# A four-layer GNN stack on one core: a new order of items on four engines, new PSUM banks and other bank waits

## What is computed

```
x = LN(x + L0(x))   # 8-head attention (head size 64); adj and exp(-adj) are added to the softmax, each times 0.33
x = LN(x + L1(x))   # hypergraph convolution 256 -> 512, ReLU, layer norm, convolution 512 -> 256, residual
x = LN(x + L2(x))   # gated diffusion: transition = adj*exp(leaky_relu(sj+si)), normalised;
                    # H = x@Wk0 + T x@Wk1 + T T x@Wk2 + biases, ReLU
x = LN(x + L3(x))   # mean over neighbours, concatenated with x, times W, ReLU
```

## Time and profile before

| | |
|---|---|
| median of three runs | 1284.12 us |
| the profiled execution | 1283.25 us |
| its span | 1281.4 us |
| PE matmul busy | 1231.0 us (96%), 9397 instructions |
| PE weight load busy | 1092.4 us (85%) |
| DVE busy | 1109.5 us (87%) |
| ACT busy | 959.2 us (75%) |
| POOL busy | 488.3 us (38%) |
| DMA | 45.14 MB, 35 GB/s over the span |
| PE's share of the chain that ended last | 80% |

### The profile page before, as it was taken

The page is one execution under the profiler, slowest core; times in us unless marked ns, Lnnn a source line. Parts: engine busy times, 40 slices in busy tenths (PEclk is TensorE's granted clock), DMA queues, the critical chain, the costliest instruction groups (busy, mean ns, idle before and its releaser), DMA issues.

```text
span 1281.4 us, 32306 instructions
## 1 busy us (share of the span) xinstructions
PE 1231.0 (96%) x9397; PEld 1092.4 (85%) x9397; DVE 1109.5 (87%) x3463; ACT 959.2 (75%) x2774; POOL 488.3 (38%) x1126
## 2 busy tenths in 40 slices
PE   4799999999999999999999999999999999999985
PEld 4588889888888888888988888898888898888874
DVE  3779889899889998988999998899898899999885
ACT  3567777778777777777777877778787777787773
POOL 2234333334343334433333444333443333344432
PEclk9889999999999999999999999999999999999998
DMA  8111101111110111111111111011111101111000
GB/s 227 30 23 40 39 21 26 30 38 38 38 28 25 28 32 38 38 38 21 25 30 38 38 38 29 25 28 32 38 38 38 23 23 30 38 38 30 16 10 9
DMA packets 146696, 45.14 MB, mean 35 GB/s; under 512 B 110577, under 2 KB 145521, under 8 KB 146673
## 3 DMA queue, kind: packets, MB, share of 16 engines
q1 hardware_dynamic: 142976, 43.81, 14.9%
q10 hardware_dynamic: 3520, 0.54, 0.3%
q0 software_dynamic: 176, 0.52, 0.2%
...
## 4 chain that ended last, share of the span: by engine, by line
PE 80%; DVE 6%; ACT 5%; issue 4%; POOL 3%; ACTq 2%; POOLq 0%; DVEq 0%
PE PS L434 13%; PE PS L435 13%; PE PS L438 13%; PE PS L563 5%; PE PS L553 5%; PE PS L509 4%; PE PS L543 4%; PE PS L510 4%; PE PS L513 4%; PE PS L598 3%; PE PS L612 2%; ACT mbc L864 2%; POOL rs L1720 1%; DVE ysb L1445 1%; ACT qk L875 1%
## 5 line engine op out<-in xcount | busy, mean ns | idle before, releaser
L1714 POOL TENSOR_TENSOR rs<-mv,eps_c 128x1 f32<-128x1 f32 x256 | 51.9, 203 | 640.3 <-DVE mv L1205 640.3
L1720 POOL TENSOR_TENSOR rs<-rs,mhalf 128x1 f32<-128x1 f32 x320 | 175.9, 550 | 25.4
L892 ACT ACTIVATE prob<-PS,neg_max 128x128 f32<-128x128 f32 x512 | 179.7, 383 | 2.0 <-DVE neg_max L1277 2.0
L509 PE MATMUL PS<-xT_hi,wqk_hi 128*128 128x256 f32 x512 | 144.5, 304 | 4.6 <-ACT wv_hi L837 4.6
L1290 DVE SCALAR_TENSOR_TENSOR prob<-prob,rl,gate 128x128 f32<-128x128 f32 x512 | 143.7, 342 | 0.1
L510 PE MATMUL PS<-xT_hi,wqk_lo 128*128 128x256 f32 x512 | 135.6, 286 | 0.0
L892 ACT ACTIVATION_READ_ACCUMULATOR prob<-PS,neg_max 128x1 f32 x512 | 114.3, 223 | 0.0
L509 PEld LDWEIGHTS PS<-xT_hi,wqk_hi 128*128 128x128 f32 x512 | 98.7, 193 | 9.9 <-issue 5.1
L1727 POOL TENSOR_SCALAR rs<-mv,rs 128x1 f32<-128x1 f32 x256 | 84.1, 329 | 53.1 <-POOL rs L1720 53.1
L513 PE MATMUL PS<-xT_lo,wqk_hi 128*128 128x256 f32 x512 | 103.9, 285 | 0.0
L510 PEld LDWEIGHTS PS<-xT_hi,wqk_lo 128*128 128x128 f32 x512 | 99.4, 194 | 0.0
...
## 6 DMA issues: line engine op xcount, KB each, us to landing
...
ablk<-in_adj_dram SPq DMA_DIRECT2D x128, 32.0 KB, 1.9
...
```

The source lines that it names most:

```text
L509: pe.matmul(dst, w[0], xT0[0][:, c], start=(c == 0), stop=False)
L892: last = act.activation(prob[:, t, h, :], PS[:, bank, k * P:(k + 1) * P], ACT.Exp, bias=neg_max[:, t, h:h + 1], accum_out=row_sum[:, t, h: ...
L1720: return pool.tensor_tensor(rs[:, n, g, 1:2], rs[:, n, g, 0:1], mhalf[:], ALU.pow)
```

## The change

It rewrites the order of items in `group` on PE, ACT, DVE and POOL, the table of PSUM banks with the extra waits that go with it, and five waits in `first()`. Items themselves, their numbers and shapes stay as they are. `out_`, `rs3_` and the second `ax_` move from the end of one step to the start of the next, so there is one more call, `group(ITERS + 1)`. Cut to its core (PE, and the ends and starts of the others):

```diff
-        bank_qk = (3, 5, 1, 5)
-        bank_v = (4, 0)
+        bank_qk = (2, 4, 0, 2)
+        bank_v = (3, 5)
         bank_AT = 2
-        bank_S = (2, 6)
-        bank_PT = (1, 3)
+        bank_S = (1, 6)
+        bank_PT = (1, 0)
         bank_PV = (6, 4)
-        bank_y0 = (0, 5)
-        bank_ax = (0, 4)
-        bank_h = (6, 0)
-        bank_hT = (1, 4)
-        bank_y1 = (5, 3)
-        bank_xT2 = 5
-        bank_Z01 = (6, 7)
-        bank_Z2 = (3, 5)
-        bank_si = (4, 1)
-        bank_T1 = (2, 7)
-        bank_T2 = (1, 1)
-        bank_xT3 = (7, 7)
-        bank_Z3 = (2, 6)
-        bank_T3 = (4, 5)
-        bank_hw = (5, 1)
+        bank_y0 = (7, 7)
+        bank_ax = (3, 6)
+        bank_h = (5, 7)
+        bank_hT = (5, 4)
+        bank_y1 = (1, 1)
+        bank_xT2 = 6
+        bank_Z01 = (0, 3)
+        bank_Z2 = (7, 5)
+        bank_si = (1, 4)
+        bank_T1 = (1, 5)
+        bank_T2 = (6, 2)
+        bank_xT3 = (6, 1)
+        bank_Z3 = (5, 6)
+        bank_T3 = (5, 7)
+        bank_hw = (0, 5)
...
                 if live(s, 1):
-                    after(pe, dve_o3, 2, s - 2, 2)
                     qk_(s, 3)
                 if live(s - 1, 0):
                     h_(s - 1, 0)
                     h_(s - 1, 1)
                 if live(s, 1):
+                    after(pe, act_qk, 4, s, 4)
                     S_(s, 0)
...
                 if live(s, 1):
+                    after(pe, dve_hb, 2, s - 1, 2)
                     S_(s, 1)
                 if live(s - 1, 0):
                     hT_(s - 1, 1)
                     hw_(s - 1, 0)
                     hw_(s - 1, 1)
+                    after(pe, act_exp, 4, s, 1)
                     y1_(s - 1, 0)
                 if live(s, 1):
                     v_(s, 0)
                 if live(s - 1, 0):
-                    after(pe, act_exp, 4, s, 2)
                     y1_(s - 1, 1)
                 if live(s, 1):
                     v_(s, 1)
                 if live(s - 1, 0):
+                    after(pe, act_exp, 4, s, 3)
                     xT2_(s - 1)
                 if live(s, 1):
                     PT_(s, 0)
                 if live(s - 1, 0):
                     Z_(s - 1, 0)
+                    after(pe, act_v, 2, s, 2)
                     Z_(s - 1, 1)
+                    after(pe, act_PT, 2, s, 1)
                     si_(s - 1, 0)
+                if live(s, 1):
+                    PV_(s, 0)
+                if live(s - 1, 0):
                     si_(s - 1, 1)
-                if live(s, 1):
-                    after(pe, act_Z1, 2, s - 1, 1)
-                    PV_(s, 0)
                 if live(s + 1, 2):
-                    after(pe, act_Z2, 2, s - 1, 1)
-                    after(pe, dve_Z2, 2, s - 1, 1)
                     qk_(s + 1, 0)
...
                 if live(s - 1, 0):
-                    after(pe, dve_z0, 2, s - 1, 2)
+                    after(pe, dve_Z2, 2, s - 1, 2)
                     T1_(s - 1, 1)
                 if live(s, 1):
-                    after(pe, act_qk, 4, s + 1, 1)
+                    after(pe, dve_Y, 2, s - 1, 1)
                     PT_(s, 1)
                 if live(s - 1, 0):
+                    after(pe, dve_OT, 2, s, 1)
                     T2_(s - 1, 0)
                 if live(s, 1):
                     W_(s, 0)
                 if live(s - 1, 0):
-                    after(pe, dve_o2, 2, s - 1, 1)
                     T2_(s - 1, 1)
...
                     Z3_(s - 1, 1)
+                    after(pe, act_za, 2, s - 1, 1)
+                    after(pe, dve_zb, 2, s - 1, 1)
                     T3_(s - 1, 0)
                 if live(s, 1):
                     AT_(s)
                 if live(s + 1, 1):
                     qk_(s + 1, 2)
                 if live(s - 1, 0):
+                    after(pe, dve_y0, 2, s, 2)
                     T3_(s - 1, 1)
...
@@ -773,7 +778,7 @@
                 qk_(0, 3)
                 pe.wait_ge(set_hi, V_DONE)
                 pe.wait_ge(set_lo, V_DONE)
-                pe.wait_ge(act_qk, 3)
+                pe.wait_ge(act_qk, 4)
                 S_(0, 0)
                 pe.wait_ge(set_hi, W1_DONE)
                 pe.wait_ge(set_lo, W1_DONE)
@@ -788,14 +793,17 @@
                 column_sums()
                 qk_(1, 0)
                 qk_(1, 1)
-                pe.wait_ge(act_qk, 5)
                 PT_(0, 1)
                 pe.wait_ge(set_wkc, 4)
+                pe.wait_ge(act_OT, 1)
+                pe.wait_ge(dve_OT, 1)
                 w3_transposes()
                 pe.wait_ge(set_hi, WOUT_DONE)
                 pe.wait_ge(set_lo, WOUT_DONE)
                 W_(0, 0)
+                pe.wait_ge(act_qk, 6)
                 PV_(0, 1)
+                pe.wait_ge(dve_y0, 1)
                 W_(0, 1)
                 gate_sums()
                 AT_(0)
@@ -813,6 +821,7 @@
                 group(s)
             group(ITERS - 1)
             group(ITERS)
+            group(ITERS + 1)
```

More of the change, by code:

```diff
@@ L989, in group @@
             def group(s):
+                if live(s - 1, 1):
+                    ax_(s - 1, 1)
+                if live(s, 1):
+                    gate_(s)
+                if live(s - 2, 0):
+                    out_(s - 2, 0)
                 if live(s, 1):
                     mask_(s)
+                if live(s - 2, 0):
+                    out_(s - 2, 1)
+                if live(s, 1):
                     qk_(s, 3)
@@ L994, in group @@
                     relu_(s - 1, 0)
[L995 to L997 removed]
+                    aT_(s - 1)
                     relu_(s - 1, 1)
@@ L1006, in group @@
                     xT2_(s - 1)
+                if live(s, 1):
+                    v_(s, 1)
+                    PT_(s, 0)
                 if live(s + 1, 2):
@@ L1460, in group @@
             def group(s):
+                if live(s - 1, 1):
+                    ax_(s - 1, 1)
+                if live(s, 1):
+                    Dsum_(s, 0)
                 if live(s - 1, 0):
-                    degb_(s - 1)
                     hb_(s - 1, 0)
@@ L1468, in group @@
                     bnh_(s - 1, 0)
+                    mvh_(s - 1, 0)
                 if live(s, 1):
@@ L1471, in group @@
                 if live(s - 1, 0):
-                    mvh_(s - 1, 0)
+                    hT_(s - 1, 0)
                     bnh_(s - 1, 1)
-                    hT_(s - 1, 0)
+                    degb0_(s - 1)
+                    hT_(s - 1, 1)
                 if live(s, 1):
@@ L1477, in group @@
                 if live(s - 1, 0):
-                    hT_(s - 1, 1)
+                    mvh_(s - 1, 1)
+                    hw_(s - 1, 0)
                 if live(s, 1):
-                    Dsum_(s, 0)
+                    rl_(s, 0, 0)
+                    max_(s, 1)
                 if live(s - 1, 0):
-                    hw_(s - 1, 0)
-                    mvh_(s - 1, 1)
-                if live(s, 1):
-                    max_(s, 1)
-                    rl_(s, 0, 0)
-                if live(s - 1, 0):
+                    y1_(s - 1, 0)
                     hw_(s - 1, 1)
@@ L1766, in group @@
             def group(s):
+                if live(s - 2, 0):
+                    rs3_(s - 2, 0)
+                    rs3_(s - 2, 1)
                 if live(s, 1):
-                    after(pool, act_x1, 2, s - 1, 2)
                     resid0_(s)
```

138 lines of the change are left out of this document (57 added, 81 removed).

## The result

The changed kernel takes 1295.07 us in the median of four runs (1294.69 to 1296.59), the kernel before 1284.36 us in four runs beside it (1283.12 to 1286.15). The ratio is 1.009, 95% interval 1.0077 to 1.0103: **slower by 0.9%**, where 1273.9 us had been forecast. The span of the profiled execution is 1294.7 us; before it was 1281.4 us. The spans differ by 13.2 us and the medians by 10.7: the profiled execution of the changed kernel is the slowest of its four, and the profiled one of the kernel before is 1.1 us faster than the median above.

What follows compares the result with a forecast made beforehand. TensorE (PE) was taken to set the pace, with only its waits winnable. From the profiled 1283.25 us, 7.8 (turns) and 2.8 (start) won and 0.4 (end) lost gave 1273.05, or 1273.9 us for the median; range 1265 to 1282 us.

Steps and rivals of the forecast that it cites:

- The wait in `S_`: `S_` of graph 0 on PE: an earlier ACT copy of quarter 3 removes a wait of 0.43 us a turn.
- The bracket's 0.15 us: Profile's own figure for the `S_` wait at 605.88; taken at its word, it caps the steady gain at 4.7 us.
- What is late next: DVE's path to the second half of `norm_`, for `PT_` of graph 0: 0.25 us earlier a turn, 7.8 us won.
- rival 3: New wait at `T1_`, as DVE's moved `mv1_` waits for POOL's scale: slower, 1291.0 us at 0.55 us; chance 0.12.
- The other waits of PE: Loop waits on PE: each new one has its producer done half a microsecond or more ahead, so cost 0.
- a wait at L655: Sign in the PE rows that, with L535 or a turn staying at 37.8 us, would show the forecast wrong.
- The start: Set-up: wait ahead of `PT_(0, 1)` and two ACT idle times go, 2.8 us won; bounds 0 and 3.3.
- The end: Last step: DVE's first `y1_` ahead of the second `hw_`, 0.4 us lost; bounds 0.5 won and 1.0 lost.
- Rival 2: Only the start wins; quarter 3 copy too late or path to `norm_` no earlier: 1281.7 us, chance 0.14.

Runs made afterwards that it cites:

- Experiment 6: On top of experiment 3, ACT copies quarter 3 of queries and keys behind the first `relu_` instead of ahead of it: 1297.04 us.
- experiment 1: Changed kernel with DVE's `Dsum_(s, 0)` moved from first in the turn to behind the first `bnh_`, away from POOL's `resid0_`: 1281.48 us.
- experiment 3: Changed kernel with both DVE moves, `Dsum_` later (experiment 1) and `mv1_` of graph 1 earlier (experiment 2): 1272.87 us.
- experiment 8: Changed kernel with POOL's `aT_` put back ahead of the first `rs1_`, `mv1_` left where the change has it: 1288.01 us.
- experiment 2: Changed kernel with DVE's `mv1_` of graph 1 put back directly behind that of graph 0: 1285.40 us.
- Experiment 9: Changed kernel with the wait for the fifth copy of queries and keys put back ahead of `PT_(0, 1)` in the set-up: 1298.28 us.
- experiment 7: Kernel before with only `Dsum_(s, 0)` moved to the front of DVE's turn, as the change has it: 1286.86 us.
- Experiment 4: Changed kernel with `Dsum_` left first on DVE and POOL's `resid0_` moved behind the first `rsh_`: 1291.03 us.

## Why the prediction was wrong

**The wait in `S_`: right.** Forecast 0.43 us a turn, measured 0.427. The bracket's 0.15 us would have made that 0.15; the starts were the better reading. The copy of quarter 3 ends 2.49 us after `h_` starts (609.20 + 0.58 - 607.29), forecast 2.71; PE wants it at 2.84. Experiment 6 shows that what is lacking of this cover costs one for one.

**"What is late next": the step that failed.** The place was right and so was the length of the path: from the low part of the second `hT_` to the second half of `norm_`, 620.55 - 615.02 = 5.53 us, forecast 5.59. What was wrong is the sentence that DVE starts this low part at 609.24. That is 7.19 us into the turn; it was 7.73 (615.02 - 607.29). PE and ACT had it ready at 7.15. DVE came late, since it had spent 1.21 us from start to start on `Dsum_`, where I had written only that "`Dsum_` is no longer among them". I had taken it out of one sum and never put it into another: of a moved item the cost at the new place is missing. With `Dsum_` at 0.2 us the starts agree (experiment 1: 7.18), and the turn of experiment 3 lies 0.30 us below that of the kernel before, where the forecast had 0.25. The prediction had the contention of DVE with POOL in hand, in rival 3, and applied it to POOL's scale alone. And the bounds of this term, 0 and 16.7 us won, left no room for a path that starts later than before.

**"The other waits of PE": wrong for `y1_`.** It was priced at 0 by producers that were early in the old timeline. `y1_` takes `hw_` from the same late DVE: 0.28 us a turn with the end of `hw_`. It went with the same move in experiment 1, so it is not a cause of its own. The waits that the change itself adds cost nothing there, as forecast.

**Rival 3, `T1_`: right in its mechanism and its place, mis-sized.** It had the path at between 0.3 us of room and a wait of 0.1; measured 0.31. The POOL part was if anything too dear (1.30 us from 625.12 to 626.42; 1.40 to 1.76 forecast). The term that was short is `norm_`: 1.05 us forecast, 1.30 from start to start (626.66 to 627.96), since `aT_` had moved on POOL to stand just there. Here too the cost at the new place was missing, this time of a POOL item. Without that (experiment 8) the wait is 0.06 us, inside the forecast. The sign that had been named, a wait at L655, shows in the starts (629.45 to 629.68) and in no bracket. And the rival alone would not have made the kernel slower: it took the failure of the step above as well, for experiment 1, with this wait in it, is slightly faster than before, and experiment 2, without it, is not.

**The start: the place right, the size in part the clock's.** Experiment 9 gives 3.2 us for the removed wait (2.8 forecast), of which about 1.7 without the lower clock. The 1.83 and 1.00 us that ACT sat idle are rows behind products that PE made in part at that lower clock. And in the profile the first `h_` is only 0.9 us earlier, and ACT's `oT` copy is at 56.93, 1.4 us earlier than 58.32, where about 3 had been forecast. PE in the set-up:

```profile
49.83 1.03 PE L553 MATMUL PS<-ident,prob 128*128 128x128 f32 x8
...
55.50 1.09 PE L563 MATMUL PS<-probT,vh 128*64 128x128 f32 x16 [0.71 <-ACT qk L884]
58.61 0.54 PE L434 MATMUL PS<-wout_hi,oT_hi 128*128 128x256 f32 x1 [2.01 <-DVE ys L1309]
```

`PT_(0, 1)` starts without a wait at 49.83. `W_(0, 1)` then waits 2.01 us for `y0_(0, 0)`, which the prediction had priced at 0. At the first `S_` the stricter wait shows as 1.79 us idle instead of 1.31, another 0.48 that was not counted. The start also varies between executions, most of all ahead of the first `S_`, which starts anywhere from 28.2 to 30.9 us in the eleven profiles. In the eight profiles of changed kernels without the wait put back, the first `h_` starts between 70.5 and 72.5 us, 71.6 in the mean, against 73.2 and 73.4 in the two of the kernel before and experiment 7. So the gain was rather 1.7 us than 0.9.

**The end: the place right, the sum of it not.** Forecast 0.4 us lost; the profile has 1.3. `y1_` of graph 1 waits 0.97 us for `hw_`, where it was 0.28:

```profile
1263.12 0.48 DVE L1348 SCALAR_TENSOR_TENSOR ysb<-PS,Dn,resid 128x256 f32<-128x256 f32 x1 [1.22 <-PE PS L612]
1263.52 0.47 DVE L1338 SCALAR_TENSOR_TENSOR hw<-PS,rs,bw_bc 128x256 f32<-128x256 f32 x1
```

```profile
1264.05 0.70 PE L612 MATMUL PS<-hw,hbh 128*128 128x256 f32 x2 [0.97 <-DVE hw L1338]
```

That is the place and about the size forecast, since on DVE `hw_` stands behind a `y1_` that waits for PE. The order can't simply be turned round, since the new table puts both `y1_` into one bank, so the second may only be written when the first has been read; other banks for it weren't tried. The steps ahead of it gave back 0.54 us: the first `y1_` starts 8.12 us after `h_`, before 8.66. What made the end long in this profile is TensorE's clock. While PE made `Z_` of graph 0, the granted clock (the third figure from the end) was 0.50, the lower of its two levels, 1.2 GHz; in experiment 9, whose code for the end is the same, it was 1.00, or 2.4 GHz, at the same place:

```profile
1267.10:1270.10 3.00, 3.00 (x10) 2.41 (x10) 0.40 (x4) 0.60 (x1) 0.46 (x2) 0.50 0.00 0
```

```profile
1270.41:1273.41 3.00, 3.00 (x18) 2.56 (x18) 0.40 (x4) 1.44 (x3) 1.22 (x4) 1.00 0.00 0
```

PE has 10 products in the first stretch and 18 in the second, and from the last `h_` to the start of `si_` the two executions differ by 1.5 us (17.95 and 16.41). From the last `h_` to the end experiment 9 takes 38.6 us and five other profiles of changed kernels 38.4 to 38.7, where the kernel before takes 39.0. (Near the very end the clock is at 0.50 for two stretches in all of them. Experiment 6 has a longer one and takes 39.6.) So without this fall of the clock the new order wins 0.4 us at the end instead of losing any. Experiment 4 has the same fall at the same place and also ends after 40.3 us; what brings it on in some executions and not in others no run here shows. As an estimate from these figures, 12.8 us lost in the turns, 1.7 won at the start and 0.4 at the end make 10.7 us, which is what the medians differ by.

**Rival 2** named the cause ("`hT_` on DVE is held by the items before it") at 1281.7 us; experiment 1, which removes this cause and keeps rival 3, ends at 1281.5. That is chance: as a rival it had no price for being held longer than before, and no floor at the old pace follows from it.
